# Layer 1 of a sparse graph attention kernel, from steps of one tile to steps of two

## The reference

```python
h = maximum(layernorm(x), 0);  x = x + gnn0(h, adj, W, a)
h = maximum(layernorm(x), 0);  x = x + gnn1(h, adj, Wq, bq, Wk, bk, Wv, bv)

def gnn1(x, adj, ...):                       # the layer that is changed
    q, k, v = x @ Wq.T + bq, x @ Wk.T + bk, x @ Wv.T + bv
    scores = where(adj > 0, q @ k.T / sqrt(128), -9e15)
    return elu(softmax(scores) @ v)
```

## Time and profile before

| | us |
|---|---|
| runs | 1947.33, 1950.41, 1957.92 (median 1950.41) |
| the profiled execution | 1946.39 |
| its span, first to last instruction | 1944.6 |
| gathers of layer 1 | 1043.03 to 1912.51 |

### The profile page before, as it was taken

How to read it: one execution, slowest core, us unless ns; L and a number is a source line. 1 busy time by engine, 2 the same in 40 slices (tenths; PEclk the granted TensorE clock), 3 DMA queues, 4 the chain that set the end, 5 groups by cost and what they waited for, 6 DMA issues and landing times.

```text
span 1944.6 us, 23228 instructions
## 1 busy us (share of the span) xinstructions
PE 1202.7 (62%) x5362; PEld 932.8 (48%) x5362; DVE 1290.0 (66%) x6912; ACT 766.3 (39%) x1507; POOL 1135.2 (58%) x1206
## 2 busy tenths in 40 slices
PE   2666767766677767766533456666565656556566
PEld 1444544443454445444433355555555555555555
DVE  4476888867898869877853455556565655556565
ACT  1966666656677758765111011111111111111111
POOL 1236666665666666665654566666666666666662
PEclk9887777777777777777555566666666666666665
DMA  9979999997999989995221112222222222222121
GB/s 307 408 283 398 389 367 350 359 330 274 368 393 388 326 315 387 384 370 180 56 53 45 44 49 55 53 54 54 49 55 53 55 54 55 54 54 54 48 56 35
DMA packets 122263, 372.41 MB, mean 192 GB/s; under 512 B 34577, under 2 KB 67858, under 8 KB 89362
## 3 DMA queue, kind: packets, MB, share of 16 engines
q1 hardware_dynamic: 75458, 289.83, 39.2%
q0 software_dynamic: 38464, 81.08, 15.5%
q10 hardware_dynamic: 8208, 0.03, 0.3%
HBM read 358.12 MB, written 12.72 MB: 191 GB/s over the span
## 4 chain that ended last, share of the span: by engine, by line
DVE 42%; another core or an unknown queue 21%; PE 13%; issue 9%; DMA 8%; ACT 3%; POOL 3%; SPq 1%; DVEq 0%; ACTq 0%; POOLq 0%
DVE arena L884 10%; DMA arena<-table,arena 6%; PE psum L1403 5%; DVE arena L1133 5%; POOL arena L580 3%; ACT arena L1184 2%; PE psum L1363 2%; DVE arena L877 2%; DMA table<-arena 2%; DVE arena L1137 2%; DVE arena L709 2%; DVE arena L902 2%; PE psum L1428 1%; DVE arena L768 1%
## 5 line engine op out<-in xcount | busy, mean ns | idle before, releaser
L580 POOL DMA_INDIRECT arena<-table,arena x576 | 555.8, 965 | 339.3 <-issue 204.7
L612 POOL DMA_INDIRECT arena<-table,arena x576 | 551.0, 957 | 327.2 <-DVE arena L893 159.5
L1184 ACT ACTIVATE arena<-arena 128x2048 bf16<-128x2048 int32 x256 | 485.7, 1898 | 58.0 <-remote 32.1
L1410 PE MATMUL psum<-arena 128*128 128x131 f32 (+1 forms) x768 | 193.1, 417 | 326.3 <-DVE arena L877 242.8
L1410 PEld LDWEIGHTS psum<-arena 128*128 128x128 f32 x768 | 160.4, 302 | 339.5 <-issue 336.4
L1363 PE MATMUL psum<-arena 128*128 128x512 bf16 x1024 | 309.4, 458 | 12.6 <-ACT arena L1184 12.6
L884 DVE SCALAR_TENSOR_TENSOR arena<-arena 128x131 f32<-128x131 f32 (+1 forms) x768 | 272.1, 354 | 18.8 <-DVE arena L884 2.2
L865 DVE TENSOR_TENSOR arena<-psum,arena 128x18 f32<-128x18 f32 x128 | 22.2, 174 | 326.9 <-remote 323.7
L1403 PE MATMUL psum<-arena 128*128 128x1 f32 x768 | 147.4, 307 | 148.0 <-DVE arena L867 137.3
L1403 PEld LDWEIGHTS psum<-arena 128*128 128x128 f32 x768 | 147.2, 273 | 181.3 <-DVE arena L867 158.5
L1320 ACT ACTIVATE arena<-psum 128x384 f32<-128x384 f32 x64 | 31.5, 492 | 425.8 <-remote 334.5
(11 more groups left out here) (199 smaller groups left out, 2112.9 us busy)
## 6 DMA issues: line engine op xcount, KB each, us to landing
arena<-in_adj_dram SPq DMA_DIRECT2D x256, 1024.0 KB
arena<-table,arena POOLq DMA_INDIRECT x1152
table<-arena POOLq DMA_DIRECT2D x32, 132.0 KB, 6.1
arena<-table SPq DMA_DIRECT2D x64, 66.0 KB
table<-arena SPq DMA_DIRECT2D x16, 256.0 KB
arena<-table SPq DMA_DIRECT2D x64, 64.0 KB
out_dram<-arena SPq DMA_DIRECT2D x16, 256.0 KB
arena<-in_x_dram SPq DMA_DIRECT2D x4, 0.5 KB, 12.2
```

The costliest lines, as they stand in the source:

```text
L580: pool.indirect_dma_start(Gt[:, v % GROUP, c + 1, :], None, table0, bass.IndirectOffsetOnAxis(idx_now[:, v % GROUP, c:c + 1], 0))\
L612: pool.indirect_dma_start(Gt[:, t % GROUP, c + 1, 0:D], None, table1, bass.IndirectOffsetOnAxis(idx_now[:, t % GROUP, c:c + 1], 0))\
L1184: nc.scalar.activation(mask[:, k, q * QUARTER:(q + 1) * QUARTER], adj_sb[:, k, q, :], ACT.Relu, accum_out=sum_all[:, bass.ds(tile, 1), q:q ...
L1410: last = nc.tensor.matmul(acc_ps[k][:, 0:width], weighted[:, c, :], Gt[:, r, OWN + c, 0:width], start=(c == 0), stop=(c == CHUNKS - 1))
```

## The change

Layer 1 goes by pairs. Each engine has one step a pair, and uses what TensorE left in PSUM in the step before. TensorE signals once at the end of its step (`tensor_step`); VectorE signals when it has read PSUM (`vector_read`), at its half (`vector_half`, which it alone waits for) and at its end (`vector_step`), and three times in between what TensorE needs in the same step (`max_done`, `slot_e_done`, `weighted_done`); ScalarE signals when it has read PSUM (`scalar_read`), once for the exponents of the over places (`over_p_done`) and at its end (`scalar_step`).

The gathered rows go to `rows`, a ring of five pairs (RING = 5) instead of `Gt` with four tiles, with their indices straight from `idx_all`. GpSimd waits once a pair, for `tensor_step` j+1 and `vector_step` j, and then issues 18 gathers; every third still waits for earlier landings. The own rows for the transpose have their own small ring `h_own`, three pairs deep. The seven instructions of `add_slot` become one multiply of 903 elements a tile and one reduction a pair. The bias matmul becomes part of a VectorE instruction. From gather to last use a pair now runs through more steps: gathered rows are scored in step j+3 and summed in step j+5, and the output is ready in step j+9. The buffers are in other places of SBUF, partly where layer 0 keeps the adjacency.

```diff
             with pool.Else():
-                pool.wait_ge(summed, T)
-                nc.gpsimd.memset(Gt[:, :, :, D:DE], 1.0).then_inc(ones_in_rows, 1)
+                nc.gpsimd.memset(rows[:, :, :, D:DE], 1.0).then_inc(ones_in_rows, 1)
...
                 for t in range(T):
-                    pool.wait_ge(summed, T + t - 3)
-                    pool.wait_ge(idx_done, T + t + 1)
+                    if t % 2 == 0:
+                        pool.wait_ge(tensor_step, t // 2 + 1)
+                        at_least(pool, vector_step, t // 2)
                     for c in range(ROWS - 1):
                         if c % BATCH == 0:
                             landed(BATCHES * (T + t) + c // BATCH - 2)
-                        pool.indirect_dma_start(Gt[:, t % GROUP, c + 1, 0:D], None, table1,
-                                                bass.IndirectOffsetOnAxis(idx_now[:, t % GROUP, c:c + 1], 0))\
+                        pool.indirect_dma_start(rows[:, t % (2 * RING), c + 1, 0:D], None, table1,
+                                                bass.IndirectOffsetOnAxis(idx_all[:, t, c:c + 1], 0))\
                             .then_inc(rows_in[t % GROUP][c // BATCH], 16)
```

SyncE waits likewise:

```diff
+                for j in range(3):
+                    sp.dma_start(h_own[:, j, :, :], pair_rows(j)).then_inc(own_in[j], 16)
+                for j in range(PAIRS):
+                    sp.wait_ge(tensor_step, j + 1)
+                    at_least(sp, vector_step, j)
+                    sp.dma_start(rows[:, 2 * (j % RING):2 * (j % RING) + 2, 0, 0:D], pair_rows(j)).then_inc(self_in[j % GROUP], 16)
+                    if j + 3 < PAIRS:
+                        sp.dma_start(h_own[:, j % 3, :, :], pair_rows(j + 3)).then_inc(own_in[j % 3], 16)
+                    if j % 2 == 0 and j >= 10:
+                        write_out(j // 2 - 5)
```

VectorE, cut to its order (p is the pair that a part is for):

```diff
+                for s in range(1, PAIRS + 9):
+                    dve.wait_ge(tensor_step, min(s, PAIRS + 7))
+                    if s >= 5:
+                        dve.wait_ge(scalar_step, min(s, PAIRS + 8) - 4)
...
+                        last = nc.vector.tensor_tensor(u_rows[:, p % 2, :, :], u_ps, two(mix_bias[:, 1, :]), ALU.add)
...
+                    if 2 <= s < PAIRS + 8:
+                        last.then_inc(vector_read, 1)
...
+                        dve.wait_ge(over_p_done, s - 4)
+                        nc.vector.tensor_tensor(owner_p[:, :, :], owner[:, p % 3, :, :], cut(p_over[:, :], P), ALU.mult)\
+                          .then_inc(weighted_done, 1)
+                        for n in range(2):
+                            last = nc.vector.tensor_tensor(weighed[:, n, :, :], rows[:, 2 * (p % RING) + n, 0:OWN, 0:DE],
+                                                           cut(p_rows[:, p % 2, n, :], DE), ALU.mult)
...
+                    last.then_inc(vector_half, 1)
+                    dve.wait_ge(vector_half, s)
+                    if in_range(s - 5):
+                        p = s - 5
+                        last = nc.vector.tensor_reduce(slot_sum[:, p % 2, :, :], weighed.rearrange("p n c d -> p n d c"), AX.X, ALU.add)
...
+                    last.then_inc(vector_step, 1)
```

TensorE:

```diff
+                for s in range(PAIRS + 7):
+                    at_least(pe, vector_read, s - 1)
+                    at_least(pe, scalar_read, s)
...
+                    if in_range(s - 4):
+                        p = s - 4
+                        pe.wait_ge(max_done, T + s - 3)
...
+                    if in_range(s - 3):
+                        p = s - 3
+                        pe.wait_ge(slot_e_done, T + s - 2)
...
+                    if in_range(s - 5):
+                        p = s - 5
+                        pe.wait_ge(weighted_done, T + s - 4)
...
+                    last.then_inc(tensor_step, 1)
```

More of the change, by code:

```diff
@@ L35 @@
 GROUP = 4
+RING = 5
+PLACES = 2 * CHUNKS
 BATCH = 3
@@ L171, in two_layer_graph_attention @@
         ident16 = place([P], BF16)
+        adj_at = top[0]
         adj_sb = place([2, QUARTERS, QUARTER], I32)
         mask = place([2, N], BF16)
+        adj_end = top[0]
         shifted = place([SEGS, P], BF16)
@@ L207, in two_layer_graph_attention @@
         m_shift = place([GROUP])
[L210 to L215, removed]
+        top[0] = early
+        scored = place([2, ROWS, DE])
+        weighed = place([2, OWN, DE])
+        assert top[0] <= layers
+        top[0] = adj_at
+        rows = place([2 * RING, ROWS, WIDTH])
+        mine_of = place([4, 2, QCOLS])
+        from_end_of = place([2, QCOLS], F16)
+        hot_of = place([3, PLACES, OVER])
+        pad_of = place([4, 2, 1 + SLOTS])
+        minus = place([1])
+        assert top[0] <= adj_end
+        h_own = place([3, 2, D])
+        h_cols = place([2, P])
+        u_rows = place([2, 2, DE])
+        owner = place([3, PLACES, P])
+        l_rows = place([2, 2, OWN])
+        l_over = place([3, PLACES])
+        slot_l = place([PLACES, OVER])
+        scores = place([2, 2, 1 + SLOTS])
+        neg_top = place([2, 2])
+        gaps = place([PLACES])
+        p_rows = place([2, 2, OWN])
+        p_over = place([PLACES])
+        owner_p = place([PLACES, P])
+        slot_sum = place([2, 2, DE])
+        row_sum = place([2, 2, DE])
+        one_over = place([3, 2])
+        sum_col = place([2, P])
+        z = place([2, 2, D])
+        z_exp = place([2, 2, D])
+        x_less = place([2, 2, D])
+        z_x = place([2, D])
         top[0] = common
@@ L341, in two_layer_graph_attention @@
         ones_in_rows = sem("ones_in_rows")
[L342 to L351, removed]
+        own_in = [sem(f"own_in{k}") for k in range(3)]
+        tensor_step = sem("tensor_step")
+        vector_read = sem("vector_read")
+        vector_half = sem("vector_half")
+        vector_step = sem("vector_step")
+        scalar_read = sem("scalar_read")
+        over_p_done = sem("over_p_done")
+        scalar_step = sem("scalar_step")
         out_written = sem("out_written")
@@ L1143, in attend @@
-                def attend(g):
-                    for b in range(GROUP):
-                        t = g * GROUP + b
-                        r, k = (b - 2) % GROUP, b % 2
-                        back, m = (b - 3) % GROUP, (b - 3) % 2
-                        if live(t, -1):
-                            publish(t + 1, (b + 1) % GROUP)
-                        if live(t, 3):
-                            weigh(T + t - 3, m, back)
-                        if live(t, 1):
-                            keep_u(t - 1, (b - 1) % GROUP)
-                        if live(t, 2):
-                            score1(t - 2, r, k, G + g + (b - 2) // GROUP + 1)
-                        if live(t, 3):
-                            for c in range(OWN):
-                                add_slot(T + t - 3, m, back, c, DE)
-                        if live(t, 2):
-                            maxima(T + t - 2, k, r)
-                        if live(t, 3):
-                            total(T + t - 3, m, DE)
-                        if live(t, 0):
-                            prepare(t, b)
-                        if live(t, 2):
-                            below(T + t - 2, k)
-                        if live(t, 4):
-                            finish(t - 4, T + t - 4, k)
```

266 lines of the change are left out of this document (158 added, 108 removed).

## The result

| | kernel before, us | changed kernel, us |
|---|---|---|
| median of four runs | 1951.41 (1947.33 to 1957.92) | 1980.24 (1967.34 to 2008.21) |
| profiled execution | 1946.39 | 1967.34 |
| its span | 1944.6 | 1965.3 |
| first gather of layer 1 to the end of the span | 901.6 | 914.4 |

The ratio is 1.0121, with a 95% interval of 1.0083 to 1.0159: 1.2% slower, where 1.6% faster was forecast. Ratios here leave out single runs far above the fastest of their kernel (the 2008.21), so medians over all runs stand beside them; by the medians it is 1.5% slower. 1980 lies in the range of 1825 to 2060; the direction is wrong.

What follows compares the result with a forecast made beforehand. Waits bound it: gather trains hold TensorE's signals. Pair 3 at 1120 plus 28 x 25.2 gives 1825.6; last release 1850.7, tail 63: span 1913.7, plus 1.8 and 4.0, 1920 us; range 1825 to 2060.

Steps and rivals of the forecast that it cites:

- That a train holds TensorE's signal to its end: Gathers of layer 1: TensorE's completion signals wait until a train ends, plus 0.14 to 0.20 us for each gather.
- forecast 2.9: Pause after a train of 18 gathers: TensorE's signal arrives 2.9 us after the train's end.
- The rate from the train of 36: Layer 1's first train before the change: signal 5.66 us after 36 gathers, giving 2.8 us for a train of 18.
- The order in a pair: Within a pair: TensorE works from 2.7 to 19 us, VectorE is done between 14 and 17, train ends at 22.2.
- The rival in which VectorE's own half-step signal is held to the release: VectorE's half-step wait: 3.5 us of work falls behind the release, pair step 28.7 us, 2018 us in all; chance 0.20.
- A pair step of 25.2 us: Layer 1's 28 steps from pair 3: train 22.2, release 2.9 and restart 0.1 us, against 27.3 before.
- the fourth rival: VectorE's multiplies hold up the gathers: train 3.1 us longer a pair, step 28.3 us, 2007 us in all; chance 0.03.
- the signal gets through: TensorE's one signal slips out during a train, so gathers bound at 22.5 us a pair: 1831 us; chance 0.17.
- another rival: Everything after the step's first 7 us waits for the release: pair step 33.2 us, 2144 us in all; chance 0.15.
- Start and tail: Layer 1's ends: first gather at 1045, three pairs in a train of 54, pair 3 at 1120, tail 63 us.
- 63 us for the steps behind the release: Tail after the last release at 1850.7: eight steps, put at 17, 13, 10, 7, 12 for four light ones, 4 last write.
- 1913.7: Forecast span of the changed kernel in us, before the 1.8 us around it and the 4.0 to the median.

Runs made afterwards that it cites:

- e3: Changed kernel with only the first ten tiles' rows gathered, later tiles computed on rows left in the ring, so work is left out: 1636.0 us.
- e4: Kernel before, with GpSimd waiting for the sum only at every second tile, so gathers come in trains of 18: 2153.5 us.
- e5: Changed kernel as it is, on a chip that ran the kernel before in 1766.5 us: 1813.6 us, ratio 1.0262 to the kernel before.
- e6: Changed kernel with VectorE's three multiplies moved to ScalarE as 20 products a pair, on e5's chip: 1793.9 us, ratio 1.0158 to the kernel before.
- e16: Kernel of e1 again, on a chip of the first kind: median 1940.4 us, ratio 0.9922 to the kernel before.
- e17: Changed kernel as it is, on e16's chip: median 1979.8 us, ratio 1.0014 to the kernel before.
- e1: Changed kernel, with GpSimd also waiting at each pair until the earlier gathers have landed: median 1967.8 us, ratio 0.9925 to the kernel before.
- e9: Kernel before, unchanged, run to see the kind of chip by its trace: 1957.8 us, a chip that holds TensorE's signals.
- e13: Kernel of e1 again, on a chip of the second kind: 1896.9 us, ratio 1.0697 to the kernel before.
- e2: Changed kernel with the old seven-instruction chain, two tiles interleaved, for the two multiplies and the reduction: ratio 0.9988 to the kernel before, layer 1 910.3 us.
- e12: Kernel of e6 again, on e9's chip: 2006.1 us, ratio 1.0278 to the kernel before.
- e11: Changed kernel with a landing wait each pair, products on ScalarE and no TensorE wait for the first pair's gathers, on e9's chip: 2003.1 us, ratio 1.0263.
- e10: Changed kernel as it is, on e9's chip: median 1982.4 us, ratio 1.0032 to the kernel before.

## Why the prediction was wrong

*That a train holds TensorE's signal to its end: right in the good pairs, too strong as a rule.* There it was 12.3 us late, with a release 2.3 us after the train (forecast 2.9). e3 shows that without gathers it is not late. But in e4, and in the joined trains, the signal came before the end of 18 gathers. The rate from the train of 36 was also misread: the 5.66 us are those of L849, which waits for `score_done`, VectorE's own signal, and VectorE had crawled until then. The forecast of 2.9 hardly changes by it. That the hold is absent on other chips I did not see and could not from one trace.

*The order in a pair: right.* TensorE was done at 13.5 us (forecast 19; it worked 10.9 us instead of 16.3, at a granted clock of 0.79 where the sum's stretch had 0.63, which explains a part), VectorE at 14.7 (forecast 14 to 17), though its reduction took 3.37 us instead of 2.0. The rival in which VectorE's own half-step signal is held to the release did not occur in the good stretch.

*A pair step of 25.2 us: the failed step.* From 1127.0, where pair 3 starts, to 1876.3, where pair 31 does (its train began at 1852.87, joined to the one before, and a train takes 23.4), are 28 steps of 26.76 us, 43.7 us more than forecast. In two parts. The first is 0.75 us a step also where all went well, 21 us: the train of 23.40 instead of 22.2, less a pause shorter by 0.5. I had weighed the Trainium skill's rule ("SBUF — State Buffer", "Who interferes with whom"), that a VectorE instruction with two SBUF inputs and a GpSimd instruction that reads SBUF shut each other out, and set it aside by the row of L877. That row shows one placing only. L877 ran from 1412.26 to 1412.81, almost wholly while this gather was under way:

```profile
1411.84 0.94 POOL L612 DMA_INDIRECT arena<-table,arena  x1 [0.30 <-issue]
```

It says nothing of a gather that starts while a multiply runs. The one at 1549.72 did, with 0.90 us of L1224 still to come, and took 1.72 us. By this trace the rule agrees in kind, but it did not hold every gather for the whole length: the two gathers beside 3.1 us of multiplies lost 1.0 us together, and the train as a whole 1.2, not the 3.1 of the fourth rival. e5 against e6 shows the price on a chip without any hold, 0.8 us a pair. So the fourth rival, to which I gave 0.03, was in part true: its sign, gathers further apart than 1.26 us beside multiplies, is there.

The second part, 22.7 us, is joined trains, a term that the sum did not have. I had "the signal gets through" as the fast rival, 1831 us, and gave it 0.17. On a chip that holds signals it is a slow case: it gets through near the end of a train, takes away the pause, and VectorE's next step falls in the crawl, whose rows I had for a train of 36 and used only in another rival. Its price is a pause of 13 to 15 us for one of 2.5, less the pause spared, 4 us a pair in the place shown. e16 against e17 shows that it decides between loss and gain: with no joined train the same kernel, with its landing wait, is 0.8% faster than before.

A slip in the recorded sum of that rival changes nothing: 1045 + 32 x 22.5 + 60 is 1825, not 1827, and 1831 is right.

*Start and tail.* Pair 3 started 7.0 us later than forecast, of which 4.8 is layer 0, which ended later in this execution (the last table write, 1030.84 before, began at 1035.67). The first train was of 54 gathers (67.2 us) with a release of 8.9 (forecast 7.2). The drain took 66.2 us from the last gather's end to the span's, forecast 65.9. That match is luck. The last train (1852.87 to 1899.11) was a joined one, and VectorE crawled to its end, so that the next step began late. In e1, where it was not joined, the same step began sooner (the changed kernel's row first, then e1's, whose last gather ended at 1907.16):

```profile
1911.88 0.43 DVE L1162 TENSOR_TENSOR arena<-psum,arena 128x258 f32<-128x258 f32 x1 [0.77 <-PE psum L1647]
```

```profile
1909.51 0.43 DVE L1165 TENSOR_TENSOR arena<-psum,arena 128x258 f32<-128x258 f32 x1 [11.60 <-remote]
```

That is 12.8 us after the last gather against 2.4, and 53.4 and 53.5 us remain from there to the end of the span. So e1's drain is 55.8 us, and 10.4 of the 66.2 us are a joined train, which the forecast did not have, while its 63 us for the steps behind the release were too many. The sum: 1913.7 + 7.0 + 43.7 + 0.6 for the last train + 0.3 = 1965.3, the measured span.

*Where the change's gain went.* In good stretches a pair takes 25.94 instead of 27.3 us, which makes 37.5 us over 28 pairs; the first three pairs, in one train, took 76.1 us (1050.9 to 1127.0) instead of 81.0 (1043.0 to 1124.0), and the last pair 1.8 less: 44 us gained. The drain gives back 34 of that (66.2 against 32.1): 24, because eight half-filled steps stand behind the last gather, and 10 for the joined train at its start. The joined trains before it took 22.7. That leaves 13 us lost, as the 914.4 against 901.6 us of layer 1 have it. Joined trains are 33 us in all, more than the loss.

What stays open: what the hold and the crawl are made of, why some chips have them, and why a signal gets through in one train and not in the next. No run took away the profiler, changed how the gathers are made, or held single gathers on purpose without the multiplies.

## What to carry to other kernels

When an engine's results come late, look at what GpSimd is doing before looking at the semaphores, and ask for a guaranteed pause rather than for the fewest ones: a signal that comes early can be worse than one that comes late, if it lets the disturbing stream run on. A deeper pipeline of bigger steps pays at its end; with 32 steps, eight of drain ate over half of the gain (24 of 44 us). Time both kernels on more than one chip before trusting a change of 1%: the changed kernel with the landing wait is 0.8% faster than the kernel before on one kind of chip here and 7% slower on the other.

## What the runs showed that I had not expected

The chips are of two kinds for this kernel. On the chips of e1, e9 and e16 and in the first comparison the kernel before takes 1951 to 1982 us at the median, on those of e5 and e13 1767 and 1772; nothing was seen in between.

In the crawl of the trains measured, starts of single instructions lie 0.7, 1.4, 2.1 or 2.8 us apart, on VectorE (joined trains) and on TensorE (e2, e12) alike. In e11 and e12, where no multiply slows a gather, it began 9 to 12 us into a train; in the joined trains VectorE was in it within a few us of its step's start. GpSimd's own pace of 1.25 us is not touched by it.

Moving the multiplies that slow a gather to ScalarE (e6's kernel) gained 1.1% on a chip that holds nothing and cost 1.2% on one that does (e12 against e10, medians 2006 and 1982). It may be that a slowed gather helps there; no run shows that apart from the move.
